# Expert stage of a four-layer kernel: the second batch's routing spread over five rounds, two norms a round later, weighting at other rounds

## The reference, cut to what matters

```python
def _L1_ffn_ref(x, Wg, Wu, Wd, Wr, temperature):
    weights = _routing_weights(x, Wr, temperature)
    gate = jnp.einsum('btd,edi->beti', x, Wg)
    up = jnp.einsum('btd,edi->beti', x, Wu)
    h = jax.nn.silu(gate) * up
    e_out = jnp.einsum('beti,eid->betd', h, Wd)
    out = jnp.einsum('bte,betd->btd', weights, e_out)
    return out

x = x + _layernorm(_L0_attn_ref(_layernorm(x), ...))
x = x + _layernorm(_L0_ffn_ref(_layernorm(x), ...))
x = x + _layernorm(_L1_attn_ref(_layernorm(x), ...))
x = x + _layernorm(_L1_ffn_ref(_layernorm(x), ...))
```

## Time and profile before

| what | value |
|---|---|
| three timed runs | 731.65, 733.98, 734.75 us; median 733.98 |
| the profiled execution | 735.22 us, span from first to last instruction 733.4 us |
| busy over the span | PE 645.0 (88%), DVE 525.5 (72%), ACT 475.8 (65%), POOL 196.6 (27%) |
| expert stage | about 624 to the end |
| mean granted clock of TensorE | 0.989 of 2.4 GHz |

### The profile page before, as it was taken

One profiled execution on the slowest core, in us unless ns is written; L12 is line 12 of the kernel. 1 busy time (PEld: TensorE's weight loads), 2 busy tenths in 40 slices (PEclk: granted clock), 3 DMA queues, 4 the chain that ended last, 5 costly groups with the idle time before them and its releaser, 6 DMA issues.

```text
span 733.4 us, 9381 instructions
## 1 busy us (share of the span) xinstructions
PE 645.0 (88%) x3336; PEld 279.5 (38%) x3370; DVE 525.5 (72%) x978; ACT 475.8 (65%) x481; POOL 196.6 (27%) x249
## 2 busy tenths in 40 slices
PE   5999899999999978988898888788898787999786
PEld 2577635446464512322232121122231111366455
DVE  5656440502707259999999999999999999675656
ACT  1244333324333269999999999999999989455221
POOL 3631100101521503465144400714600015040002
PEclk9999999999999989999999999999999989999999
DMA  9000200000220621106122511111011104400441
GB/s 317 4 1 1 70 20 0 1 0 1 62 68 0 173 65 55 43 13 182 55 55 55 142 47 49 55 55 55 20 35 55 55 19 99 115 0 1 117 144 30
DMA packets 32255, 42.78 MB, mean 58 GB/s; under 512 B 5200, under 2 KB 19280, under 8 KB 31824
## 3 DMA queue, kind: packets, MB, share of 16 engines
q1 hardware_dynamic: 32208, 42.17, 19.6%
HBM read 31.60 MB, written 10.55 MB: 57 GB/s over the span
## 4 chain that ended last, share of the span: by engine, by line
PE 41%; ACT 23%; DVE 21%; issue 11%; SPq 2%; DMA 1%; POOL 1%; DVEq 0%; POOLq 0%; ACTq 0%
ACT w_hh L997 18%; PE ps L700 7%; PE ps L715 6%; DVE hid L1293 5%; DVE hid L1288 5%; PE ps L745 4%; PE ps L687 4%; PE ps L625 3%; PE ps L606 2%; PE ps L501 2%; PE ps L532 2%; PE ps L754 2%; ACT probs L969 2%; PE ps L727 1%; DVE st L1099 1%
## 5 line engine op out<-in xcount | busy, mean ns | idle before, releaser
L997 ACT ACTIVATE w_hh<-hid 128x2048 f32<-128x2048 f32 x128 | 249.9, 1952 | 9.0 <-DVE hid L1293 8.5
L625 PE MATMUL ps<-w_hh,v_h 128*32 128x512 f32 x1024 | 138.6, 613 | 32.4 <-ACT w_hh L997 31.1
L606 PE MATMUL ps<-q_s,k_s 64*128 64x512 bf16 x256 | 99.9, 391 | 15.4 <-DVE hid L1288 15.0
L1288 DVE TENSOR_TENSOR hid<-ps,probs 128x1024 f32<-128x1024 f32 x86 | 104.6, 1216 | 5.5 <-ACT probs L969 2.6
L1293 DVE SCALAR_TENSOR_TENSOR hid<-ps,probs 128x1024 f32<-128x1024 f32 x86 | 104.7, 1217 | 4.7 <-PE ps L606 3.5
L606 PE MATMUL ps<-q_w,k_w 64*128 64x512 bf16 x256 | 99.9, 391 | 0.8 <-DVE hid L1293 0.7
L969 ACT ACTIVATE probs<-ps 128x1024 f32<-128x1024 f32 x86 | 91.3, 1061 | 4.6 <-PE ps L606 4.6
L606 PE MATMUL ps<-q_g,k_s 128*128 128x512 bf16 x222 | 71.2, 390 | 9.2 <-issue 5.6
L1195 DVE SCALAR_TENSOR_TENSOR hid<-ps,s_b,rot 128x512 f32<-128x512 f32 x16 | 11.9, 750 | 85.2 <-ACT rot L938 85.2
L606 PEld LDWEIGHTS ps<-q_w,k_w 64*128 64x128 bf16 x256 | 23.6, 93 | 108.9 <-issue 55.3
L700 PE MATMUL ps<-hid,w_hh 128*128 128x512 f32 x128 | 56.3, 595 | 0.0
(11 more groups left out here) (296 smaller groups left out, 1011.9 us busy)
## 6 DMA issues: line engine op xcount, KB each, us to landing
qk_rows<-part SPq DMA_DIRECT2D x48, 128.0 KB, 2.3
w_hh<-w_rows SPq DMA_DIRECT2D x4, 1024.0 KB, 9.5
qk_rows<-part_g SPq DMA_DIRECT2D x24, 128.0 KB, 2.3
q_g<-qk_rows SPq DMA_DIRECT2D x32, 96.0 KB, 2.2
k_s<-qk_rows SPq DMA_DIRECT2D x32, 96.0 KB, 2.3
k_w<-qk_rows SPq DMA_DIRECT2D x32, 96.0 KB, 2.4
q_s<-qk_rows SPq DMA_DIRECT2D x32, 96.0 KB, 2.5
q_w<-qk_rows SPq DMA_DIRECT2D x32, 96.0 KB, 2.6
```

The lines of the kernel that those rows point to most:

```text
L606: last = mm(ps[:, base + half, :], k_op[rows, u, keys], q_op[rows, u, half * CHUNK:(half + 1) * CHUNK], start=True, stop=True)
L625: last = mm(ps[VW * g4:VW * g4 + VW, 6, :], v_h[:, u, mt, :], ee[:, mt % 2, g4 * CHUNK:(g4 + 1) * CHUNK], start=(mt == 0), stop=(mt == BT ...
L997: A(ee[:, mt % 2, :], zz[:, mt % 2, :], ACT.Exp).then_inc(S["e"], 1)
L1288: v.tensor_tensor(zz[:, mt % 2, 0:SEQ], banks[:, 2 * CHUNK:4 * CHUNK], gg[s % 3], ALU.add).then_inc(S["z1"], 1)
```

## The change

Three tables and some conditions move. `LAST_DOWNS` starts at round 27 instead of 28; `weighted_after` is a table from round 11 on. Weightings per round: rounds 11 to 14 two instead of one, 15 to 18 none instead of one, 19 and 20 one as before, 25 to 29 two each, 30 three and 31 three (before: two in rounds 27 to 29, six in 30, four after the loop). The steps of the second batch's routing take rounds 15 to 19 instead of 15 to 17. ScalarE's norms of chunks 0 and 1 and VectorE's adds come a round later, the statistics stay; the statistics of chunk 2 come in round 30 instead of after the loop, and its add stands before the last chunk's statistics. GpSimd no longer works out the bias of the last half.

```diff
-LAST_DOWNS = {28: 2, 29: 4, 30: 6}
+LAST_DOWNS = {27: 2, 28: 4, 29: 6, 30: 8}
+WEIGHTED = {11: 8, 12: 10, 13: 12, 19: 15, 20: 16, 25: 18, 26: 20, 27: 22, 28: 24, 29: 26, 30: 29, 31: ND}
...
-    return min(downs_after(min(n + 1, ND - 1)), n + 1)
+    if n <= 10:
+        return downs_after(n + 1)
+    return max(count for at, count in {**WEIGHTED, 14: 14}.items() if at <= n)
...
-                if n == 19:
+                if n == 20:
                     pe.wait_ge(S["xt_d"], 2)
                     turn_weights(1).then_inc(S["wtp_d"], 1)
...
-                if n == 19:
+                if n == 20:
                     d_wt(1)
-                if n in (21, 24):
-                    c = (n - 21) // 3
+                if n in (22, 25):
+                    c = (n - 22) // 3
                     norm("d_out", c, sum_d(c), y_d(c)).then_inc(S["o_ap"], 1)
...
                 if n == 16:
                     route_b(1)
+                if n == 17:
                     route_rank(1)
-                if n == 17:
+                if n == 18:
                     route_c(1)
+                if n == 19:
                     route_d(1)
                 if n in (20, 23):
                     d_out_stats((n - 20) // 3)
-                if n in (22, 25):
-                    d_out_add((n - 22) // 3)
-            for m in range(weighted, ND):
-                d_weight(m)
-            d_out_stats(2)
-            last_stats(0)
+                if n in (23, 26):
+                    d_out_add((n - 23) // 3)
+                if n == 30:
+                    d_out_stats(2)
             d_out_add(2)
-            last_stats(1)
+            for half in range(2):
+                last_stats(half)
...
-            for half in range(2):
-                scale_and_bias(len(NORMS) - 1, len(NORMS) + half, slice(2 * half, 2 * half + 2))
+            scale_and_bias(last, last + 1, slice(0, 2))
+            pool.wait_ge(S["stats"], last + 2)
+            me.step(g.tensor_scalar(rs[:, last, 2:CT], mv[:, last, 2:CT, 1], LN_EPS, None, ALU.add))
+            g.tensor_tensor(rs[:, last, 2:CT], rs[:, last, 2:CT], half_down[:, 2:CT], ALU.pow).then_inc(S["rstd"], 1)
```

More of the change, by code:

```diff
@@ L1821, in scale_and_bias @@
                 g.tensor_tensor(nb[:, i, tiles], nb[:, i, tiles], rs[:, i, tiles], ALU.mult).then_inc(S["rstd"], 1)
-            for i in range(NORMS.index(("c_out", 2)), len(NORMS) - 1):
+            last = len(NORMS) - 1
+            for i in range(NORMS.index(("c_out", 2)), last):
                 scale_and_bias(i, i + 1, slice(0, CT))
-            for half in range(2):
-                scale_and_bias(len(NORMS) - 1, len(NORMS) + half, slice(2 * half, 2 * half + 2))
+            scale_and_bias(last, last + 1, slice(0, 2))
+            pool.wait_ge(S["stats"], last + 2)
+            me.step(g.tensor_scalar(rs[:, last, 2:CT], mv[:, last, 2:CT, 1], LN_EPS, None, ALU.add))
+            g.tensor_tensor(rs[:, last, 2:CT], rs[:, last, 2:CT], half_down[:, 2:CT], ALU.pow).then_inc(S["rstd"], 1)
 _OUTS = (BATCH, SEQ, P)
```

## The result

The changed kernel takes 727.3 us (median of four runs, 726.38 to 728.09) against 733.5 before (four runs, 731.65 to 734.75): ratio 0.990, 95% interval 0.9885 to 0.992. The forecast was 726.9 in a range of 724.6 to 729.6, with a chance of 0.94 on faster by over 0.5%. Set against the kernel before in later runs, the same kernel gave 0.990 again (0.988 to 0.992).

What follows compares the result with a forecast made beforehand. No engine is full; TensorE's stops, waiting for other engines, bound the expert stage. Gains 3.10 + 2.46 + 0.67 + 1.2 = 7.4, less 0.3 for the port, give 7.1: from 733.98 to 726.9 us, range 724.6 to 729.6.

Steps and rivals of the forecast that it cites:

- the four stops named: TensorE's waits: 2.14 us before down(12), 1.38 before down(13), 1.07 before up(24), 1.77 before up(27).
- Part 1: Second batch's routing without weighting beside it, up to up(21): gain 3.10 us, with a new 0.9 stop before the transpose.
- Part 2: Norms a round later, up(21) to up(27): gain 2.46 us, two stops removed, a new 0.80 stop before up(26).
- Part 3: Weighting and downs a round sooner, up(27) to the last sixteen matmul pairs: gain 0.67 us.
- The tie at the last weighting: VectorE's weighting 31 ends at 716.27, the last sixteen matmul pairs start at 716.32; lateness there costs one for one.
- Part 4: The tail: earlier add of chunk 2 gives 0.83, shorter GpSimd chain some 0.6, some 0.2 lost; gain 1.2 us.
- the shared port: GpSimd's chunk 2 norm, slowed beside weightings 29 to 31, pushes the first half of the last statistics by 0.3 us.
- So GpSimd is held up by VectorE, not VectorE by it.: Read from rows before the change: GpSimd's power took 1.35 us meeting a weighting; a weighting inside a power kept 0.68.
- VectorE is held up by GpSimd: Rival: a power blocks a weighting once in the last rounds, 1.04 plus 0.25; 728.2 us, chance 0.08.
- The stop only moves: Rival: TensorE waits for routing's later end, and a late first norm, giving 2 to 4 back; 729 to 731, chance 0.08.
- copies late: Rival: the routing weights' copies take 10 us instead of 6.3, delaying weighting 16; 727 to 730, chance 0.03.
- sign for a slower clock: Rival: TensorE falls to 1.2 GHz from 685 on, about 738, chance 0.02; sign: 0.6 us matmuls where 0.3 is usual.

Runs made afterwards that it cites:

- a_routing_back: Changed kernel with routing back in rounds 15 to 17, weightings of rounds 11 to 20 one each, transpose in round 19; stage 102.71 us, ratio 0.994.
- b_norms_back: Changed kernel with ScalarE's norms back in rounds 21 and 24 and VectorE's adds back in 22 and 25; stage 101.91 us, ratio 0.992.
- d_downs_back: Changed kernel with only LAST_DOWNS back, so downs of chunk 2 start a round later while the weighting stays early; stage 101.06 us, ratio 0.991.
- g_pool_busy: Changed kernel plus eight unused, chained GpSimd subtractions of 128x512 beside the weightings of rounds 26 to 29; stage 100.60 us, ratio 0.990.
- f_turn_21: Changed kernel with the transpose of the routing weights and its copy in round 21 instead of 20; stage 99.04 us, ratio 0.989.
- h_routing_alone: Kernel before with only the routing's part of the change, its weightings and transpose included; stage 104.01 us, ratio 0.9955.
- j_norms_alone: Kernel before with only the norms moved to rounds 22 and 25 and the adds to 23 and 26; stage 104.75 us, ratio 0.997.

## Why the prediction was right, and where it was not

- **What bounds the stage** (stops of TensorE, not the load of an engine): right. Each of the four stops named went, and a_routing_back and b_norms_back brought each pair back alone (the one before up(24) as 0.75 and not 1.07).
- **Part 1, 3.10.** Measured 2.94 by the two profiles (up(21) 688.12 against 683.96 + 1.22); taken back alone 3.12, alone in the kernel before 3.21. The new stop before the transpose was put at 0.9 and its bracket says 0.75, yet up(21) came 0.16 later than forecast (683.96 + 1.22 = 685.18 against 685.02): a bracket counts from the modelled end of the matmuls, the forecast from start to start, and by starts the stop is no shorter. The routing ended at 684.93 against 684.84.
- **Part 2, 2.46.** Measured 2.58: up(27) stands 73.11 after up(0) (694.13 + 1.72), before 78.63, 5.52 less in all. The stop before up(26), forecast 0.80, was 0.56 from start to start: statistics and add together held VectorE 1.78, not 1.91. Up(25) was forecast without a stop and lost 0.12 at its tie: the four ups from 686.57 take 7.00 and not 4 x 1.72 = 6.88.
- **Part 3, 0.67.** Measured 0.56. The tie at the last weighting was met: it ends 0.16 ahead of the last sixteen in the changed kernel (715.09 against 715.25), and in the two kernels where it came later, d_downs_back and g_pool_busy, they stand 0.20.
- **Part 4 and the shared port, 1.2 - 0.3 = 0.9.** Measured 1.55. This is the mis-sized term, and it was off in each of its pieces. The 0.3 for the port did not show. It did to GpSimd what was said (its power 1.35, below), and the add of chunk 2 ended at 718.69 in the clock of before, where 718.8 had been forecast; but the last sixteen began 0.15 later than forecast, so the first half of the last statistics was pushed by 0.08 and not 0.3. The second half starts 3.77 behind the last sixteen, 0.99 sooner than the 4.76 of before, and not 0.83. From there to VectorE's end it is 3.31 against 3.87, a gain of 0.56 where 0.6 - 0.2 = 0.4 was put. GpSimd's work on the last half takes 1.01 (719.89 to 720.90) instead of 1.78, and the first half did not hold it up: it starts 0.09 behind the statistics in both kernels. What is lost again, 0.2, is lost on VectorE: its scaling starts 0.25 behind GpSimd's end, because the first half's add (720.80) stands in front of it, and before, in the row below, it started 0.04 behind.
- **The step that was wrong in kind:** "So GpSimd is held up by VectorE, not VectorE by it." It holds for a power of 128x4 and is false in general, as g_pool_busy shows. Here it did no harm, since GpSimd has only small operations in this stage. One row on a small operation was stretched to a rule.

VectorE's scaling of the last half in the kernel before:

```profile
729.99 0.73 DVE L1565 TENSOR_SCALAR y_a<-ps,mv,rs 128x128 f32<-128x128 f32 x2 [1.19 <-POOL nb L1821]
```

GpSimd in the changed kernel, for chunk 2's norm beside weightings 29 to 31, and for the last half:

```profile
713.43 1.35 POOL L1824 TENSOR_TENSOR rs<-rs,half_down 128x4 f32<-128x4 f32 x1
714.86 0.29 POOL L1825 TENSOR_TENSOR nb<-nb,rs 128x4 f32<-128x4 f32 x1
...
719.89 0.22 POOL L1832 TENSOR_SCALAR rs<-mv 128x2 f32<-128x2 f32 x1
720.19 0.71 POOL L1833 TENSOR_TENSOR rs<-rs,half_down 128x2 f32<-128x2 f32 x1
```

The power at 713.43 takes 1.35 where 1.04 is usual; VectorE's three weightings over it ran at their normal pace of 0.60 each. For the last half the chain is now two operations, 719.89 and 720.19.

Of the rivals, "VectorE is held up by GpSimd" didn't come: those three weightings show it. The prediction prices it at 1.0 in one place (a sum of about 6.1) and at 1.29 in the other (728.2); in no run does a power hold up a weighting. "The stop only moves" was right in that a stop appeared at the transpose and wrong in its size; "copies late" had 2.7 us of room, which f_turn_21 used up. The granted clock stayed at 1.00, the 2.4 GHz level, from up(0) to the last matmul; one window of the changed kernel, laid out as the earlier trace rows:

```profile
686.00:703.00 17.00, 16.60 (x68) 9.30 (x67) 11.59 (x27) 7.33 (x16) 4.21 (x8) 1.00 0.93 275
```

TensorE is busy 16.60 of 17.00 us there, against 14.16 in the earlier trace rows. The prediction's sign for a slower clock, matmuls of 0.6 us where 0.3 is usual, is good for the 128x128 ones alone (275 ns on average from 686 on); those of 128x512 take 598 ns at the full clock.

The sum was 7.1 and the stage gave 7.63. The time from median to median gave 6.2 or, in the later runs, 8.3; both hold the scatter of the rest of the program. That the measured 727.3 lies 0.4 from the forecast of 726.9 is thus in part luck; the stage is what bears the forecast out.

## What to carry to other kernels

When no engine is full, list the stops of the engine with the most work, and for each ask what stands **in front** of the instruction waited for in its own engine's queue, not how long that instruction takes: here moving work by a round or two, and leaving out two small operations of GpSimd, gave 1%, and no instruction was made faster. A moved piece wants a place where its engine waits anyway (weighting 14 behind hidden(16), while the exponentials run); two pieces between the same two products make the next stop. Read such changes from a stage of the profile with a fixed start, not from the whole time, when they are worth less than the rest of the program scatters.

## What the runs showed that I had not expected

- **The stage repeated to 0.05 us, while the 620 us ahead of it vary by 5.** The first figure is from the two profiles of the changed kernel. Over all 14 profiles up(0) starts between 620.61 and 625.52, in programs that are the same up to there. The earliest is d_downs_back, whose row of granted clock has no dip (mean 1.000); the latest is h_routing_alone with 0.95 in the window of 200 to 300 and 0.98 in that of 500 to 600, 0.989 over the whole. The windows of the earliest and of the latest, with the granted clock as the third number from the end:

```profile
200.00:300.00 100.00, 92.26 (x424) 41.64 (x423) 55.32 (x94) 56.87 (x55) 26.16 (x28) 1.00 0.24 69
```

```profile
200.00:300.00 100.00, 93.19 (x397) 39.98 (x396) 52.81 (x89) 54.06 (x53) 25.93 (x26) 0.95 0.25 71
```

  The clock isn't all of it (f_turn_21 has 0.993 and starts at 624.32), and what else moves was not tried.
- **GpSimd and VectorE exclude each other by operation, but not for a small one**: two weightings 1.28 alone and up to 2.37 beside 128x512 subtractions, 0.68 unchanged inside a 128x4 power of 1.04. Why the small one doesn't block is open.
- **A GpSimd operation of four columns can be 0.2 or 0.7 us long** depending on whether a weighting on VectorE has just begun: 0.67 in d_downs_back (begun 0.07 before it), 0.20 in f_turn_21 (begun 0.13 after it) and 0.20 in j_norms_alone (none). Between d_downs_back and j_norms_alone this moved a stop on TensorE by 0.46.
